# Edge sort of a graph network on one Trainium2 core: the column one-hots laid out with the group's edges innermost

## The reference, cut to what matters

```
xn = layernorm(x)
gathered = edge_weight[:, None] * xn[dst]           # 100,000 edges
agg = segment_sum(gathered, src, num_segments=6250)
x = x + (agg @ W.T + b) + linear_attention(xn)
x = x + moe(layernorm(x))                            # 8 experts, 2 for each node
```

## Time and profile before

| what | us |
|---|---|
| median of the runs | 2456.24 |
| the profiled execution's own time | 2455.17 |
| its span | 2453.4 |
| POOL busy in the span | 1416.4 |
| DVE busy in the span | 1447.1 |
| the sort: first column comparison to the end of the last scatter | 107.8 to 307.0 |
| of it, POOL's scatters | 117.8 to 307.0 |

### The profile page before, as it was taken

How to read it: one execution, slowest core, us unless ns; L and a number is a source line. 1 busy time by engine, 2 the same in 40 slices (tenths; PEclk the granted TensorE clock), 3 DMA queues, 4 the chain that set the end, 5 groups by cost and what they waited for, 6 DMA issues and landing times. The chain is left out here.

```text
span 2453.4 us, 52311 instructions
## 1 busy us (share of the span) xinstructions
PE 1673.7 (68%) x13546; PEld 1207.5 (49%) x13546; DVE 1447.1 (59%) x3501; ACT 1291.2 (53%) x4201; POOL 1416.4 (58%) x1346
## 2 busy tenths in 40 slices
PE   6776446666666566666654544445459999999998
PEld 3565324444444445445442211213357777777776
DVE  7998535555555565555554654556764555555554
ACT  6455245555555555555555655555505656665654
POOL 3688846666666666666666666665353444444444
PEclk8999868888887788888886565555569999999999
DMA  4022144444444443333333334543502222232232
GB/s 144 18 82 77 50 134 131 130 130 126 130 131 121 135 117 99 99 100 99 101 88 88 88 86 129 148 130 113 156 15 49 49 48 47 49 50 47 47 49 32
DMA packets 140257, 224.62 MB, mean 92 GB/s; under 512 B 34054, under 2 KB 94672, under 8 KB 139954
## 3 DMA queue, kind: packets, MB, share of 16 engines
q0 software_dynamic: 67040, 146.22, 23.4%
q1 hardware_dynamic: 73042, 76.15, 10.4%
HBM read 181.40 MB, written 41.82 MB: 91 GB/s over the span
## 5 line engine op out<-in xcount | busy, mean ns | idle before, releaser
L961 POOL DMA_INDIRECT misc<-z_d,consts x902 | 857.9, 951 | 525.1 <-issue 254.4
L1206 DVE SCALAR_TENSOR_TENSOR acc<-ps,consts,acc 128x256 f32 x902 | 434.3, 481 | 545.4 <-remote 471.5
L1286 PE MATMUL ps<-misc 128*128 128x256 f16 x565 | 185.8, 329 | 272.7 <-DVE acc L1206 152.7
L1752 ACT ACTIVATE misc<-ps,misc 128x128 f32<-128x128 f32 x840 | 239.3, 368 | 239.1 <-PE ps L1717 164.8
L1793 POOL DMA_INDIRECT out<-misc,pos x105 | 167.0, 1591 | 289.8 <-ACT misc L1817 253.9
L985 ACT ACTIVATE rec<-rec,misc 128x128 f16<-128x128 f16 x674 | 228.5, 392 | 193.3 <-DVE rec L1067 115.5
L1717 PE MATMUL ps<-misc,big 128*128 128x128 f16 x1680 | 327.1, 220 | 0.0
L1715 PE MATMUL ps<-misc,big 128*128 128x128 f16 x1680 | 326.9, 220 | 0.2
L1716 PE MATMUL ps<-misc,big 128*128 128x128 f16 x1680 | 326.6, 219 | 0.0
L1732 PE MATMUL ps<-big,rec 128*128 x840 | 319.6, 381 | 0.0
L985 ACT ACTIVATE misc<-rec,misc 128x128 f16<-128x128 f16 x678 | 228.9, 391 | 166.1 <-DVE rec L1067 113.6
(11 more groups left out here) (334 smaller groups left out, 3833.0 us busy)
## 6 DMA issues: line engine op xcount, KB each, us to landing
big<-in_w2T SPq DMA_DIRECT2D x60, 256.0 KB
misc<-z_d,consts POOLq DMA_INDIRECT x902
big<-xT_d SPq DMA_DIRECT2D x98, 128.0 KB
big<-in_w1T SPq DMA_DIRECT2D x32, 256.0 KB
tok_d<-misc SPq DMA_DIRECT2D x50, 132.0 KB, 1.9
xT_d<-misc SPq DMA_DIRECT2D x49, 128.0 KB
z_d<-misc SPq DMA_DIRECT2D x49, 128.0 KB
acc<-in_x SPq DMA_DIRECT2D x1, 6144.0 KB
```

The costliest lines, as they stand in the source:

```text
L961: e.indirect_dma_start(out=rows[k], out_offset=None, in_=c.z_d, in_offset=bass.IndirectOffsetOnAxis(ap=idx[u][:, k:k + 1], axis=0)).then_i ...
L1206: e.scalar_tensor_tensor(out=rows_of, in0=out_ps[t % BG], scalar=c.gain, in1=rows_of, op0=ALU.mult, op1=ALU.add).then_inc(s_add[k], 1)
L1286: e.matmul(o, w[:, 0, :], rows[k][:, 0:D], start=True, stop=False)
L1752: l = e.activation(hidden[:, m, :], h_ps[u][:, m, :], ACT.Relu, bias=b1x[u][:, m:m + 1])
```

## The change

The column one-hots are stored column by column with the 28 edges innermost, like the slot one-hots, and are compared with a table of 32x28 entries instead of 32. ScalarE reads them through a turned view (a step of 28 elements, 56 bytes, between neighbouring columns) and writes its masks in the old order. Sizes and the count of instructions stay.

```diff
-    col_hot = [matrix(ring.take(SC * GT, F16), GT, SC) for _ in range(2)]
+    col_hot = [matrix(ring.take(SC * GT, F16), SC, GT) for _ in range(2)]
...
-    col_no = nos.take(SC, F16)
+    col_no = matrix(nos.take(SC * GT, F16), SC, GT)
...
-            iota(col_no, [[1, SC]])
+            iota(col_no, [[1, SC], [0, GT]])
...
             def column(s):
-                across = lambda a: a.rearrange("p (n a) -> p n a", a=1)
-                e.tensor_tensor(col_hot[s.u % 2], one(col_no).to_broadcast([P, GT, SC]),
-                                across(col16[:, part_of(s.i * GT, GT)]).to_broadcast([P, GT, SC]), ALU.is_equal).then_inc(s_col, 1)
+                e.tensor_tensor(col_hot[s.u % 2], col_no, one(col16[:, part_of(s.i * GT, GT)]).to_broadcast([P, SC, GT]),
+                                ALU.is_equal).then_inc(s_col, 1)
...
-                e.activation(matrix(masks[s.u % 2], GT, SC), col_hot[s.u % 2], ACT.Copy, scale=65535.0).then_inc(s_mask, 1)
+                e.activation(matrix(masks[s.u % 2], GT, SC), col_hot[s.u % 2].rearrange("p c n -> p n c"), ACT.Copy, scale=65535.0).then_inc(s_mask, 1)
```

## The result

The changed kernel takes 2462.98 us in the median of 20 runs (2457.86 to 2466.5), the kernel before 2457.12 in 20 runs beside them (2453.12 to 2460.09). The ratio is 1.0023, with a 95% interval of 1.0017 to 1.0029: 0.2% slower, where 0.1% faster was forecast. The time lies inside the stated range and on the other side of no change.

What follows compares the result with a forecast made beforehand. POOL's 112 scatters were taken to bound the sort. Head 0, phase gain -5.5 and loss +2.5 gave -3.0 us against 2455.17: 2452.2, or 2453.2 as the median; eight-in-ten range 2446 to 2465.

Steps and rivals of the forecast that it cites:

- What bounds the stage: The sort: it ends when POOL has issued 112 scatters; DVE's time isn't on that path by itself.
- The comparison: DVE's column comparison L506: from 1081 to 614 ns, 13.1 us less over 28, none of it directly on the path.
- The table: POOL's iota for the larger column table: 0.94 us instead of about 0.1, covered, so no cost.
- ACT's mask: ScalarE's L585, reading at 56 bytes: 0.36 us more than 0.94, covered before the product L516 starts.
- the high bound of 1.30: Most the turned read was taken to add to a mask, from ACT's row writing at 8 bytes: 1.30 us for 896 elements.
- the sign that I had named: Sign of being wrong: the mask L585 passes 1.6 us; 0.94 to 1.3 was expected.
- the least cover of 0.55: Time from the mask's end to L516's start: 0.55 us at least, 0.9 and more in most steps.
- the turned read delays the product: Rival: a mask over 0.6 us longer delays L516, whose scatter is held longer; +8 to +18, 2464 to 2474; chance 0.15.
- What it is worth on the path: Scatters' starts against L514: 15 distances gain 5.5 us, three lose 2.5, 8 waiting steps don't move; sum -3.0.
- The head: Before the first scatter, behind two masks and the first eviction: -0.5 to +2.1 us, taken as 0.
- A premise of the working: A scatter begun during such a DVE instruction waits until that ends, then runs 0.91 us undisturbed beside the next.
- DVE's time counts after all: Rival: the 13.1 us saved on DVE come out in full, 2443; chance 0.06.

Runs made afterwards that it cites:

- e6_blocks_of_4: The changed kernel with only four edges innermost in the column one-hots, so ScalarE reads at a step of 8 bytes; ratio to before 0.9993.
- e1_steps: The kernel before plus nine ScalarE reads of 896 elements at various steps in idle time behind the last eviction; one run, 2457.91 us.
- e2_slow_compare: The changed kernel with its column table in 32 bits instead of 16, which puts the comparison back to 1084 ns; ratio to before 1.0016.
- e5_mask_twice: The kernel before with ScalarE doing each dense mask twice, first into a spare tile; ratio 1.0018.
- e7: The kernel before with each of DVE's 49 low halves computed twice, first into one spare tile with a semaphore of its own; ratio 1.0123.
- e8: The kernel before with each column comparison done twice, first into a spare tile; ratio 1.0236.
- e10: The kernel before with each low half and each mask done twice; ratio 1.0117.
- e12: The kernel before with each low half computed twice, the second copies going to two spare tiles in turn, without a semaphore; ratio 1.0122.
- e9: The kernel before with one swap in ScalarE's stream, mask(i+1) ahead of norm(i+1); ratio 1.0004.
- e3_turn_in_pe: The changed kernel with masks and products keeping edges innermost, so PE instead of ScalarE reads with the 56-byte step; ratio to before 1.0385.

## Why the prediction was wrong, point by point

- *What bounds the stage*: right. POOL issues 112 scatters without a wait in the kernel before and in the changed one. A DVE saving of 13 us is worth nothing by itself (e6_blocks_of_4, 0.9993).
- *The comparison*, 614 ns: right, 618. *The table*: right; the two iotas took 4.74 instead of 3.87 us and their reader had cover.
- *ACT's mask*: this is the step that failed. I took 0.36 us more, from PE's weight load as the nearest row; it is 0.86 (1802 against 940), between that and the high bound of 1.30; the sign that I had named, L585 beyond 1.6 us, came. Of the least cover of 0.55 only 0.40 could be used, since a product that waits starts 0.15 behind the mask's end (145.37, 145.52). So 0.36 would just have been hidden, and 0.86 is 0.46 too much, against a lateness of 0.43 in the step shown. The earlier slots' comparison didn't shrink the least cover, as I had allowed for, but brought more steps down to it: "most steps have 0.9 and more" was 15 of 28, and 12 of 28 in e1_steps. The rival "the turned read delays the product" is what happened, with its mechanism as written: later product, longer hold, +6.8 us in the product. Its price at 0.9, +8 and 2464 us, is close to the 2462.98 measured, with some luck: it took 0.3 in 28 steps, and 19 products were late, by 0.37 on average. I gave it 0.15. The row that I set against it, L594, reads from PSUM and says nothing on SBUF. On this the Trainium skill (Advanced Engine Details and Errata, SBUF Cachelines) was right where my choice of row was wrong: it says that an access that stays in its 16-byte line runs at full speed, that two hits in a line are needed for it, and that changing the line with each access pays. The trace of e1_steps agrees: 0.99 us at 8 bytes, where two reads fall into a line, and 1.77 at 16, where one does.
- *What it is worth on the path*, -3.0 us of phase: not found. The steps that I worked out behave so: 0.74 held instead of 1.19 with two blocks (0.82 by the forecast), 1.60 instead of 0.80 with one (1.64 by the forecast). But 10 steps and not 15 gained, and 4 and not 3 lost, which makes -1.2; the slots hold 1.1 less in the changed kernel and 1.0 more in e6_blocks_of_4, and two traces of the sort before differ by 1.6. Counting only steps without a wait and leaving the others as they were was not enough, since a faster DVE waits in other steps.
- *The head*, 0: +0.8 by the trace (118.61 against 117.78). Of that 0.25 is that the sort itself started later (108.07 against 107.82); the rest fits two longer masks ahead of the first eviction, less what the comparison and the wait gave back.
- The sum by what was measured is 0.8 + 6.8 - 1.1 = 6.5, against the 6.7 by which the last scatter is later. e2_slow_compare and e5_mask_twice reach 1.0016 and 1.0018 with the longer mask and the slow comparison; their products hold 3.5 and 2.8 us more, about half of the changed kernel's 6.8, and their first scatter comes 1.3 us later behind the first comparison, where the changed kernel's comes 0.6 later.
- A premise of the working held in the kernels that it was used for and is not a law: that a scatter is released at the next boundary between two DVE instructions. e7, e8, e10 and e12 hold some longer, and then to the end of the whole run of `tensor_tensor`, three instructions or in e8 four, and not to a boundary between. What decides between the two stays open. It isn't when the mask ends (e9, e10) nor an added semaphore (e12); a busier DVE is common to all four. The rival "DVE's time counts after all" is thus refuted for time taken from DVE here, and not for time added to it.

## What to carry to other kernels

Before a view with a step is given to an engine that has slack on average, compare its time in that one instruction with the cover in front of its reader: 0.86 us more on an engine that is half idle made 19 products late by 0.37 us on average, and that cost 6.8 us, while 13 us saved on the other engine were worth nothing. When a layout is good for one engine and bad for the other, a blocked one (runs of four 16-bit elements here) gave both their cheap form. Where POOL's indirect DMAs bound a stage, as here, DVE's busy time alone tells little: 13 us taken away gave nothing, and 23 us added cost 30. Look at where its instructions with two SBUF inputs stand against POOL's.

## What the runs showed of the hardware

- ScalarE reads 896 elements from SBUF in 0.95 us at steps of 2 and 4 bytes, 0.99 at 8, and 1.72 to 1.80 at 16, 32 and 56, with 16 and with 32 bits alike. VectorE keeps its fast rate of comparison (621 ns for 896) with inner runs of only four elements.
- TensorE pays for a step in a matmul's moving operand too: with 128 columns at a step of 56 bytes a matmul took 403 ns (e3_turn_in_pe), with dense ones 227, and 28 in a row took 6.44 us instead of 1.99. The price was the same at a granted clock of 1.00 and of 0.50.
- A scatter's descriptors wait for DVE's `tensor_tensor` with both inputs in SBUF, 16-bit or 32-bit, at either rate (1.63 to 2.15 us, and 0.96 alone), and not for a `scalar_tensor_tensor` whose first input is in PSUM. The wait ends at the next boundary between two DVE instructions, or, in e7, e8, e10 and e12 for 54 scatters, only with the last `tensor_tensor` in a row. The Trainium skill (SBUF — State Buffer, Who interferes with whom) has such an instruction contend with GpSimd's reads and infers that the making of descriptors is spared. Here it is not: 0.96 us alone, 2.15 and up to 6.36 beside such instructions.
